# A graph, mixer and wavelet layer on one core: edge pairs spread over 24 mlp turns, finishing steps begun with the last of them, and a 512-wide product in three one-pass parts

## The chip, the cores and the metric

One core of a Trainium2 chip runs the whole layer. The metric is the device time of one execution in microseconds. Engines are named PE (matmul), DVE (vector), ACT (scalar), POOL (GpSimd) and SP (the queue that issues plain DMAs). Each engine works through its own list in order, and engines wait for each other by semaphores.

## The reference, cut to what matters

The layer has 6250 rows of 512 numbers and 100,000 edges from `dst` to `src`.

```python
xn = layernorm(x)
hidden = relu(xn @ W1 + b1)                     # graph part, 256 wide
h = hidden @ W2 + b2
x = x + h + segment_sum(h[dst], src) + mixer(xn)   # mixer: random-feature attention, then
                                                   # an mlp: gelu(norm(y) @ w1 + b1) @ w2 + b2
ll = haar_low_band(layernorm(x))
delta = fc2(gelu(fc1(interp(ll)))) - ll
x = x + layernorm(x) + haar_inverse_of(delta)
```

As `h` is linear behind the relu, the kernel sums `hidden` over the edges first and multiplies the sums by `W2` once for each row.

## The kernel before

The 6250 rows stand in 125 partitions, 50 tiles; a step is two tiles, so each pass over the rows has 25 steps (`STEPS`). Pass 1 computes keys, the `hidden` rows (stored to DRAM as the table `hidden_rows`) and sorts the edges. The sorted edges are then worked off in 440 pairs (`PAIRS`), each a pair of 128 edges that belong to one tile of 125 rows. For a pair POOL issues two indirect DMAs (`gathers`, L609), which fetch 2 x 128 rows of the table into one of 12 places of a ring (`RING`); ACT makes 0/1 matrices from the edges' row numbers (`one_hots`, L1272 and L1276, four pairs at a time); PE multiplies (`groups`, L876 to L879); DVE adds the result to the tile's sums in `acc` (`add_groups`, L1732). These four do their work between the steps of passes 2 and 3, so many pairs at each place of a step.

Pass 2 (attention, step 2 in what follows) has 25 steps with 8 pairs each. After it comes a loop over turns v. In turn v the mlp of step a = v is computed as long as there is one (`transposes` L970, `features` L983, `mlp2` L992 on PE; `norm_rows` L1292, `gelus` and `copy_hT` L1182 on ACT; `skip_rows` L1856, L1858 and `z_rows` L1866 on DVE), and step b = v - `LAG` is finished, when there is one. In the finishing of a step its sums are transposed (`acc_transposes`, L1016), copied by ACT (`copy_accT`, L1327), multiplied by `W2` (`w2_products` L1024 into banks that are free while mlp turns run, later `x1_products` L1057, which adds onto what `x1_opened`, L1049 and L1051, has put into the bank); DVE takes the row statistics (`x1_rows`, L1890 to L1897), POOL the inverse roots (`roots`, L618), DVE the low band (`ll_rows`, L1903 to L1917); then follow `ll_transposes` (L1067), `fc1` (L1075), `fc2` (L1085), ACT's `scaled_rows` (L1350) and DVE's `out_rows` (L1925, L1931). A turn works on three steps at once: it transposes and multiplies the sums of step b + 2 (b + 1 in mlp turns), takes the statistics of step b + 1 and finishes step b.

`pair_counts` deals the pairs to the turns. Step t may be finished once 390 + 2t + 2 pairs are in. Before, 22 turns of 8 bring 176 pairs, so that `LAG` is 23: turns 0 to 21 are mlp alone, turns 22, 23 and 24 are mixed (mlp and finishing), turns 25 to 47 are the tail, finishing alone (b = 2 to 24). Turns 22 to 24 have 8 pairs too, the first six of the tail 4 each. In POOL's list a turn's `gathers` stand before its `roots`:

```python
gathers(TURN + sum(SECOND) + BETWEEN + sum(THIRD[:v]) + soon + RING)
if 0 <= b + 1 < STEPS:
    roots(steps[b + 1])
```

## Time and profile before

| | |
|---|---|
| three runs | 1779.51, 1782.45, 1791.55 us; median 1782.45 us |
| the profiled execution | 1781.86 us, span 1780.0 us |
| granted TensorE clock, mean | 0.969 of full speed |
| pass 2, steady steps | about 600 to 980 us |
| mlp turns 0 to 21 | about 1016 to 1470 us |
| mixed turns 22 to 24 | about 1470 to 1568 us |
| tail turns, b = 2 to 24 | about 1569 to 1780 us |

A timeline row gives start and length in us from the start of the span, the engine, the source line, the operation and its output and inputs; in brackets stands how long the engine had been idle and who released it. "PE" rows of fp32 matmuls count two for each matmul written in the code. A turn is told by its first row of one kind: the copy `L1182` marks mlp turns (late in the turn), the transposes `L1067` the start of a tail turn.

### The profile page before, as it was taken

The page shows a single profiled execution, that of the slowest core. Times are in us where ns is not written, and L with a number is a line of the kernel's source. Part 1 is how long each engine was busy: PE and PEld are TensorE (multiplying, and loading weights), DVE is VectorE, ACT ScalarE, POOL GpSimd, SP SyncE. Part 2 cuts the span into 40 slices and gives each one's busy share as a digit, 9 for nine tenths or more (in the row PEclk, how much of TensorE's full clock was granted, in tenths as well). Part 3 has the DMA queues.
Part 4 walks back from the last instruction along what each step waited for, and adds up shares of the span by engine and source line. Part 5 has one row for each costly group of instructions (what it writes and reads, how often), then busy time and mean ns, then how long its engine had stood idle before and what let it go on. Part 6 is the DMA issues. An engine that isn't in the chain of part 4 may idle for free.

```text
span 1780.0 us, 24848 instructions
## 1 busy us (share of the span) xinstructions
PE 1625.4 (91%) x8131; PEld 1224.3 (69%) x8131; DVE 1035.9 (58%) x2321; ACT 818.5 (46%) x1890; POOL 1036.6 (58%) x1129
## 2 busy tenths in 40 slices
PE   4999999998899999999999699999999988789996
PEld 3778877787677788888877476666666665556554
DVE  5899999996255555565565233333333334357776
ACT  2135444444244344554454465555554554435442
POOL 3023444343777777777777777777777777553010
PEclk9999999999899999999999699999999999889998
DMA  6023222222356556656655755555565655444332
GB/s 191 12 75 123 87 87 87 87 88 89 114 156 202 175 173 189 184 177 187 185 177 150 233 170 169 187 172 179 176 183 178 181 180 172 130 136 141 127 131 81
DMA packets 87425, 263.61 MB, mean 148 GB/s; under 512 B 18765, under 2 KB 20813, under 8 KB 87298
## 3 DMA queue, kind: packets, MB, share of 16 engines
q0 software_dynamic: 43456, 119.44, 24.1%
q1 hardware_dynamic: 43842, 142.59, 23.6%
q8 instruction: 67, 1.10, 0.2%
q14 instruction: 60, 0.49, 0.1%
HBM read 217.15 MB, written 44.80 MB: 147 GB/s over the span
## 4 chain that ended last, share of the span: by engine, by line
PE 49%; POOL 15%; DVE 14%; issue 9%; DMA 8%; ACT 3%; DVEq 0%; POOLq 0%; ACTq 0%
POOL sb_weights L609 12%; PE bank L983 6%; DVE sb_weights L1452 6%; DMA sb_weights<-hidden_rows,sb_weights 5%; PE bank L992 5%; PE bank L931 4%; PE bank L901 2%; PE bank L903 2%; PE bank L902 2%; PE bank L1057 2%; PE turn_bank L877 2%; PE bank L877 2%; DMA sb_step<-x_t 2%; DVE sb_step L1633 2%; PE bank L726 1%
## 5 line engine op out<-in xcount | busy, mean ns | idle before, releaser
L609 POOL DMA_INDIRECT sb_weights<-hidden_rows,sb_weights x880 | 862.0, 980 | 298.8 <-issue 244.4
L1732 DVE TENSOR_TENSOR sb_acc<-sb_acc,bank 125x257 f32 x220 | 92.6, 421 | 345.6 <-PE bank L879 301.5
L1272 ACT ACTIVATE sb_weights<-sb_const,sb_weights 128x125 f16<-128x125 f16 x880 | 266.5, 388 | 50.9 <-PE turn_bank L879 49.7
L992 PE MATMUL bank<-sb_weights,sb_step 128*125 128x512 f32 x400 | 188.4, 616 | 10.0 <-issue 8.5
L983 PE MATMUL bank<-sb_weights,sb_step 128*128 128x250 f32 x800 | 184.8, 384 | 10.3 <-issue 8.0
L983 PEld LDWEIGHTS bank<-sb_weights,sb_step 128*128 128x128 f32 x800 | 151.1, 194 | 33.3 <-issue 15.6
L1452 DVE TENSOR_TENSOR sb_weights<-sb_weights 128x512 f32<-128x512 f32 (+3 forms) x256 | 164.3, 683 | 3.6
L1732 DVE TENSOR_TENSOR sb_acc<-sb_acc,turn_bank 125x257 f32 x220 | 92.5, 420 | 107.1 <-PE turn_bank L879 85.9
L576 POOL TENSOR_SCALAR sb_const<-sb_const 125x2 f32<-125x2 f32 x25 | 9.5, 381 | 240.0 <-ACT sb_step L1174 240.0
L1190 ACT ACTIVATE sb_step<-sb_step 125x256 f32<-125x256 f32 x100 | 48.2, 502 | 215.3 <-DVE sb_step L1625 214.7
L725 PE MATMUL bank<-sb_w_parts,sb_x_high 128*125 128x512 f32 (+1 forms) x400 | 139.0, 348 | 0.0
L992 PEld LDWEIGHTS bank<-sb_weights,sb_step 128*125 128x125 f32 x400 | 74.3, 195 | 89.0 <-issue 86.9
L726 PE MATMUL bank<-sb_w_parts,sb_x_high 128*125 128x512 f32 (+1 forms) x400 | 135.1, 338 | 0.0
L727 PE MATMUL bank<-sb_w_parts,sb_x_low 128*125 128x512 f32 (+1 forms) x400 | 134.9, 337 | 0.0
L1276 ACT ACTIVATE sb_weights<-sb_weights,sb_const 128x1000 f16<-128x1000 f16 x110 | 124.1, 1128 | 3.6
L738 PE MATMUL bank<-sb_w_parts,sb_x_high 128*125 128x256 f32 (+1 forms) x300 | 102.7, 342 | 16.7 <-DVE sb_step L1633 14.1
L1306 ACT COPY sb_step<-bank 128x500 f32<-128x500 f32 x25 | 14.4, 576 | 190.5 <-PE bank L919 190.5
L618 POOL TENSOR_TENSOR sb_step<-sb_step,sb_const 125x2 f32<-125x2 f32 x25 | 17.5, 698 | 142.7 <-DVE sb_step L1897 142.6
L931 PE MATMUL bank<-sb_const,sb_step 128*125 128x512 f32 x200 | 95.6, 601 | 0.0
L876 PE MATMUL turn_bank<-sb_weights 128*125 128x257 f16 x220 | 63.0, 287 | 35.4 <-DMA sb_weights<-hidden_rows,sb_weights 29.0
L739 PE MATMUL bank<-sb_w_parts,sb_x_high 128*125 128x256 f32 (+1 forms) x300 | 94.6, 315 | 0.0
L740 PE MATMUL bank<-sb_w_parts,sb_x_low 128*125 128x256 f32 (+1 forms) x300 | 94.6, 315 | 0.0
(310 smaller groups left out, 3632.2 us busy)
## 6 DMA issues: line engine op xcount, KB each, us to landing
sb_step<-x SPq DMA_DIRECT2D x63, 500.0 KB
sb_step<-x_t SPq DMA_DIRECT2D x50, 500.0 KB, 6.7
sb_weights<-hidden_rows,sb_weights POOLq DMA_INDIRECT x880, 4.5
y_rows<-sb_step SPq DMA_DIRECT2D x25, 500.0 KB
sb_step<-y_rows SPq DMA_DIRECT2D x25, 500.0 KB
z_rows<-sb_step SPq DMA_DIRECT2D x25, 500.0 KB
sb_weights<-z_rows SPq DMA_DIRECT2D x13, 500.0 KB
out<-sb_weights SPq DMA_DIRECT2D x13, 500.0 KB
```

The lines of the kernel that those rows point to most:

```text
L609: pool.indirect_dma_start(out=ring[:, n % RING * 2 + h, 0:HID], out_offset=None, in_=table, in_offset=bass.IndirectOffsetOnAxis(ap=row_of[ ...
L725: pe.matmul(bk, high, rhs(0, c), start=c == 0, stop=False)
L726: pe.matmul(bk, high, rhs(1, c), start=False, stop=False)
L727: mm = pe.matmul(bk, low, rhs(0, c), start=False, stop=c == KC - 1)
L738: pe.matmul(outs[c], high, first, start=c == 0, stop=False)
L931: mm = pe.matmul(banks[m][0:P, :], qpT[:, c, m * P:(m + 1) * P], pmat[:, c, :], start=False, stop=c == KH - 1)
L983: last = pe.matmul(bk[:, (c % 2) * 250:(c % 2) * 250 + 2 * P], mlp1_w[:, k, c * 128:(c + 1) * 128], hT3[:, t.s, k, :], start=k == 0, stop= ...
L992: mm = pe.matmul((BC, BD)[m][0:P, :], gT3[:, k, m * P:(m + 1) * P], mlp2_w[:, k, :], start=k == 0, stop=k == KC - 1)
L1272: mm = act.activation(hit[q % 2][:, i, :], iota_h[:, :], ACT.Abs, bias=less_lane[:, q * BP + i // 2, i % 2:i % 2 + 1])
L1276: act.activation(hit[q % 2], hit[q % 2], ACT.Relu, scale=-1.0, bias=one_c[:, 0:1]).then_inc(hits, 1)
L1452: sort_op(dve.tensor_tensor(half(target, c, lo), a, b, op))
L1732: dve.tensor_tensor(dst, dst, (BE, BH)[n % 2][0:P, 0:RW], ALU.add).then_inc(g_add, 1)
```

## The change

Three things are changed.

1. The 176 pairs that must be in before a step can be finished are spread over 24 turns of seven or eight pairs (7, 7, 8, 7, 7, 8, ...), so `LAG` is 25. Turns 0 to 23 are mlp alone, turn 24 is the one mixed turn and only begins finishing (b = -1: sums of steps 0 and 1, statistics and low band of step 0), and turns 25 to 49 are the tail, b = 0 to 24. Turn 24 has 8 pairs, the first ten turns of the tail 4 each. ACT makes the 0/1 matrices by a rule (`hits_until`) instead of two batches a turn.
2. The product of the sums with `W2` is made of one-pass products (fp32 data read as F32R): the weights are split once into a high and a low part (`late_weights`), the sums in each step: ACT's copy becomes the high part, and a new DVE instruction `sums_low` subtracts it from the bank for the low part. PE then does high x high, high x low and low x high, 12 instructions of 512 columns in place of 4 full fp32 matmuls.
3. PE waits for the low part (`a_low`) where it waited for the copy (`a_t`): before the product, and before `fc2`, whose bank is the one that the sums were read from. Tiles move to other places (`fc1e`, `fc2_w`, `t4`, `accT`), and `fc2_w` is loaded one wait later.

```diff
 def pair_counts():
     turn, second, between = 8, [8] * STEPS, 8
-    start, third, lag = turn + sum(second) + between, [], 1
-    while start + sum(third) < PAIRS - NT + 2:
-        third.append(min(8, PAIRS - NT + 2 - start - sum(third)))
-    lag = len(third) + 1
+    start, lag = turn + sum(second) + between, STEPS
+    third = spread(PAIRS - NT + 2 - start, lag - 1)
     while start + sum(third) < PAIRS:
         third.append(min(8 if len(third) < STEPS else 4, PAIRS - start - sum(third)))
...
-SLOT = [0, 1, 2, 0, 6] + [(5, 4, 3, 1, 2, 0, 6)[u % 7] for u in range(STEPS - 5)]
+SLOT = [(0, 1, 2, 6, 5, 4, 3)[u % 7] for u in range(STEPS)]
...
+            def sums_product(bk, m, opened):
+                for c in range(KH):
+                    high, low = (v[:, c, m * P:(m + 1) * P].bitcast(F32R) for v in (accT, acc_low))
+                    w_high, w_low = (v[:, c, :].bitcast(F32R) for v in (gnn2_high, gnn2_low))
+                    pe.matmul(bk, high, w_high, start=c == 0 and not opened, stop=False)
+                    pe.matmul(bk, high, w_low, start=False, stop=False)
+                    mm = pe.matmul(bk, low, w_high, start=False, stop=c == KH - 1)
+                return mm
...
             def x1_products(t):
-                pe.wait_ge(a_t, t.u + 2)
+                pe.wait_ge(a_low, t.u + 2)
                 for m in (0, 1):
-                    for c in range(KH):
-                        mm = pe.matmul(x1_of(t, m), accT[:, c, m * P:(m + 1) * P], gnn2_w[:, c, :],
-                                       start=False, stop=c == KH - 1)
+                    mm = sums_product(x1_of(t, m), m, True)
                 mm.then_inc(a_mm, 1)
...
             def fc2(t):
...
                 if t.u + LAG >= STEPS:
-                    pe.wait_ge(a_t, min(STEPS, t.u + 3) + 1)
+                    pe.wait_ge(a_low, min(STEPS, t.u + 3) + 1)
...
+            def hits_until(n):
+                while next_hits[0] < BATCHES and BP * (next_hits[0] - 1) <= n:
+                    one_hots(next_hits[0])
...
                     gelus(steps[a], 0)
-                    one_hots(2 * STEPS + 5 + 2 * a)
+                    hits_until(ahead)
...
                     gelus(steps[a], 1)
-                    one_hots(2 * STEPS + 6 + 2 * a)
+                    hits_until(ahead + sum(counts[0:2 if a == 2 else 3]))
...
+            def sums_low(t):
+                dve.wait_ge(a_t, t.u + 2)
+                dve.tensor_tensor(acc_low.rearrange("p a b -> p (a b)").bitcast(F32R), sums_bank(t)[:, 0:500],
+                                  accT.rearrange("p a b -> p (a b)"), ALU.subtract).then_inc(a_low, 1)
...
                     if b + 1 < STEPS:
                         x1_rows(steps[b + 1])
+                    if b + 2 < STEPS:
+                        sums_low(steps[b + 2])
                     add_groups(counts[0] + counts[1])
```

POOL, from the first gather to the fourth of its `roots` (the line of `roots` is L618 before and L621 after; 812 gathers are 406 pairs). Before:

```order
L609 DMA sb_weights<-hidden_rows,sb_weights 128x256 x812
L618 TENSOR_TENSOR sb_step<-sb_step,sb_const 125x2
L609 DMA sb_weights<-hidden_rows,sb_weights 128x256 x16
L618 TENSOR_TENSOR sb_step<-sb_step,sb_const 125x2
L609 DMA sb_weights<-hidden_rows,sb_weights 128x256 x16
L618 TENSOR_TENSOR sb_step<-sb_step,sb_const 125x2
L609 DMA sb_weights<-hidden_rows,sb_weights 128x256 x12
L618 TENSOR_TENSOR sb_step<-sb_step,sb_const 125x2
```

and after:

```order
L612 DMA sb_weights<-hidden_rows,sb_weights 128x256 x812
L621 TENSOR_TENSOR sb_step<-sb_step,sb_const 125x2
L612 DMA sb_weights<-hidden_rows,sb_weights 128x256 x12
L621 TENSOR_TENSOR sb_step<-sb_step,sb_const 125x2
L629 COPY sb_step<-sb_const 128x125 x2
L632 COPY sb_step<-sb_acc 125x2
L612 DMA sb_weights<-hidden_rows,sb_weights 128x256 x8
L621 TENSOR_TENSOR sb_step<-sb_step,sb_const 125x2
```

The same 812 gathers stand ahead of the first roots; behind them 16, 16, 12 and three times 8 have become 12 and seven times 8.

PE, a tail turn without gathers, from its first transposes into the product (before):

```order
L1067 MATMUL bank2<-sb_const,sb_step 128x125 x2
L1016 MATMUL bank1<-sb_const,sb_acc 128x125 x4
L1049 MATMUL bank0<-sb_weights,sb_step 125x512
L1075 MATMUL bank2<-sb_step,sb_weights 128x125 x4
L1049 MATMUL bank3<-sb_weights,sb_step 125x512
L1085 MATMUL bank1<-sb_weights,sb_step 125x256 x2
L1031 MATMUL bank2<-sb_const,sb_step 126x125 x2
L1057 MATMUL bank0<-sb_weights 125x512 x2
L1057 MATMUL bank3<-sb_weights 125x512 x2
```

and after:

```order
L1019 MATMUL bank1<-sb_const,sb_acc 128x125 x4
L1059 MATMUL bank0<-sb_weights,sb_step 125x512
L1083 MATMUL bank2<-sb_step 128x125 x4
L1059 MATMUL bank3<-sb_weights,sb_step 125x512
L1093 MATMUL bank1<-sb_step 125x256 x2
L1041 MATMUL bank2<-sb_const,sb_step 126x125 x2
L1027 MATMUL bank0<-sb_w2_parts 125x512
L1028 MATMUL bank0<-sb_w2_parts 125x512
L1029 MATMUL bank0<-sb_w2_parts 125x512
```

The order is the same; the four full products at the end are now the three rows L1027 to L1029, four times over (twice for bank0, twice for bank3).

DVE, a tail turn without gathers, from the statistics to the low band (before):

```order
L1890 BN_STATS sb_const<-bank5 125x6
L1890 BN_STATS sb_const<-turn_bank 125x6
L1892 TENSOR_SCALAR sb_const<-sb_const 1x1
L1894 BN_AGGR sb_step<-sb_const 125x2 x2
L1897 TENSOR_SCALAR sb_step<-sb_step 125x2
L1903 SCALAR_TENSOR_TENSOR sb_step<-sb_step 125x2
L1905 TENSOR_SCALAR sb_step<-sb_step 125x2
```

and after:

```order
L1911 BN_STATS sb_const<-bank5 125x6
L1911 BN_STATS sb_const<-turn_bank 125x6
L1913 TENSOR_SCALAR sb_const<-sb_const 1x1
L1915 BN_AGGR sb_step<-sb_const 125x2 x2
L1918 TENSOR_SCALAR sb_step<-sb_step 125x2
L1897 TENSOR_TENSOR sb_w2_parts<-bank1,sb_w2_parts 128x500
L1924 SCALAR_TENSOR_TENSOR sb_step<-sb_step 125x2
```

The subtraction of `sums_low` (after: L1897) stands where DVE hands the variances to POOL and next waits for POOL's roots.

## Rows read from the trace of the kernel before

**Rows 1.** The page: busy time of each engine, share of the span

```profile
PE 1625.4 (91%) x8131; PEld 1224.3 (69%) x8131; DVE 1035.9 (58%) x2321; ACT 818.5 (46%) x1890; POOL 1036.6 (58%) x1129
```

**Rows 2.** The gathers (L609) in two stretches: window, length, busy us, count, PEclk, DMA, GB/s

```profile
1034.00:1259.67 225.67, 172.06 (x177) 0.98 0.58 177
1259.67:1466.88 207.21, 157.85 (x163) 0.98 0.60 179
```

**Rows 3.** What PE waited for, 1180 to 1460 us: total, times, longest

```profile
PE turn_bank L876 <- DMA sb_weights<-hidden_rows,sb_weights: 18.9, 13, 2.2
```

**Rows 4.** Timeline, hT copies of mlp turns 0, 1, 2 and 21: start, length, engine

```profile
1034.01 0.57 ACT L1182 COPY sb_weights<-bank 128x500 f32<-128x500 f32 x1 [4.59 <-PE bank L970]
...
1052.51 0.57 ACT L1182 COPY sb_weights<-bank 128x500 f32<-128x500 f32 x1 [4.59 <-PE bank L970]
...
1079.16 0.57 ACT L1182 COPY sb_weights<-bank 128x500 f32<-128x500 f32 x1 [8.53 <-PE bank L970]
...
1466.88 0.57 ACT L1182 COPY sb_weights<-bank 128x500 f32<-128x500 f32 x1 [6.29 <-PE bank L970]
```

**Rows 5.** Timeline, turns 22 to 24, the mixed ones

```profile
1493.76 0.74 POOL L618 TENSOR_TENSOR sb_step<-sb_step,sb_const 125x2 f32<-125x2 f32 x1
...
1494.53 0.16 DVE L1903 SCALAR_TENSOR_TENSOR sb_step<-sb_step 125x2 f32<-125x2 f32 x1 [11.21 <-POOL sb_step L618]
...
1498.20 0.44 PE L876 MATMUL bank<-sb_weights 128*125 128x257 f16 x1 [6.84 <-DVE sb_acc L1732]
...
1518.63 2.04 PE L992 MATMUL bank<-sb_weights,sb_step 128*125 128x512 f32 x2 [4.23 <-issue]
...
1568.17 1.04 PE L1016 MATMUL bank<-sb_const,sb_acc 125*128 125x125 f32 x4
```

**Rows 6.** Timeline, the start of tail turns 2, 6, 8 and 23

```profile
1578.77 0.38 PE L1067 MATMUL bank<-sb_const,sb_step 125*128 125x125 f32 x2
...
1621.49 0.38 PE L1067 MATMUL bank<-sb_const,sb_step 125*128 125x125 f32 x2
...
1642.06 0.38 PE L1067 MATMUL bank<-sb_const,sb_step 125*128 125x125 f32 x2
...
1760.09 0.38 PE L1067 MATMUL bank<-sb_const,sb_step 125*128 125x125 f32 x2
```

**Rows 7.** Timeline, POOL's roots in tail turns 2, 3 and 4

```profile
1580.89 0.71 POOL L618 TENSOR_TENSOR sb_step<-sb_step,sb_const 125x2 f32<-125x2 f32 x1 [8.29 <-DVE sb_step L1897]
...
1593.62 0.72 POOL L618 TENSOR_TENSOR sb_step<-sb_step,sb_const 125x2 f32<-125x2 f32 x1 [0.71 <-DVE sb_step L1897]
...
1604.81 0.72 POOL L618 TENSOR_TENSOR sb_step<-sb_step,sb_const 125x2 f32<-125x2 f32 x1
```

**Rows 8.** Timeline, tail turn 9, without gathers (1649.94 to 1657.82 us)

```profile
1650.78 0.57 ACT L1327 COPY sb_weights<-bank 128x500 f32<-128x500 f32 x1
...
1651.80 0.17 DVE L1897 TENSOR_SCALAR sb_step<-sb_step 125x2 f32<-125x2 f32 x1
...
1652.77 0.16 DVE L1903 SCALAR_TENSOR_TENSOR sb_step<-sb_step 125x2 f32<-125x2 f32 x1 [0.80 <-POOL sb_step L618]
...
1653.20 1.13 PE L1085 MATMUL bank<-sb_weights,sb_step 128*125 128x256 f32 x4
...
1654.39 3.60 PE L1057 MATMUL bank<-sb_weights 128*125 128x512 f32 x8
...
1658.02 1.30 DVE L1890 BATCH_NORM_STATS2 sb_const<-bank 125x6 f32<-125x512 f32 x2 [0.67 <-PE bank L1057]
```

**Rows 9.** Timeline, one-pass matmuls in step 2, and a sum from PSUM

```profile
722.56 0.40 PE L902 MATMUL bank<-sb_w_parts,sb_x_high 128*125 128x512 f32 x1
...
724.87 0.40 PE L903 MATMUL bank<-sb_w_parts,sb_x_low 128*125 128x512 f32 x1
...
1477.39 0.69 DVE L1886 TENSOR_TENSOR sb_weights<-sb_weights,bank 125x512 f32<-125x512 f32 x1 [4.59 <-PE turn_bank L1024]
```

**Rows 10.** Timeline, rows of an mlp turn that wait for a load

```profile
1281.60 1.52 ACT L1292 ACTIVATE sb_step<-sb_step,sb_const 125x512 f32<-125x512 f32 x2 [0.51 <-DMA sb_step<-y_rows]
```

40 lines of the change are left out of this document (25 added, 15 removed).

## The prediction

> **What bounds the kernel now.** I read the page first: PE is busy 91% of the span and every other engine under 60% [rows 1]. So PE sets most of the time, and the question is where it doesn't. The waits by stage and the timeline turn by turn give three regimes.
>
> In the mlp turns PE waits for gathered rows: 18.9 us in 13 waits between 1180 and 1460 us [rows 3]. POOL issues them without a pause, 163 in 207.21 us, that is 1.271 us each or 2.54 us a pair [rows 2]; the stretch before has 1.275. Eight pairs are 20.3 us. Turns 0 to 21 take (1466.88 - 1034.01) / 21 = 20.6 us each [rows 4]. Where enough rows lie ready a turn with eight pairs takes 18.50 us (turn 0 to turn 1), and turn 2, with its extra products for the fc weights, 26.65 us [rows 4]. POOL's issue rate is the bound here, and PE has 2 us to spare a turn.
>
> In the mixed turns the engines wait for each other. POOL computes the first roots only behind its 812th gather, at 1493.8 us; DVE has by then waited 11.21 us for them, and PE, which waits for DVE's adds, 6.84 us [rows 5]. In the next turn PE stands 4.23 us behind ACT (the gelu of `fc1` is queued behind a batch of 0/1 matrices) [rows 5]; turn 24 shows the same. The end of turn 22 lies at about 1499.9 us (PE resumes at 1498.2 and has two pairs' products, eight of 0.44 us overlapping by half). From there to 1568.17 us, where the last mlp turn ends [rows 5], two turns take 68.3 us.
>
> In the tail, turns without pairs last (1760.09 - 1642.06) / 15 = 7.87 us [rows 6], and PE is full: its eight product rows alone start at 1654.39 and DVE gets them at 1658.02 [rows 8]. DVE needs 7.21 of these 7.87 us (it idles 0.67 at the end of its turn), 0.80 of it waiting for roots [rows 8]. Turns with pairs are longer: where POOL still gathers, its roots are 1604.81 - 1593.62 = 11.19 us apart (8 x 1.27 us of gathers and 1.0 us for roots and the degree copy) [rows 7]; behind the last gather the two turns from 1621.49 to 1642.06 us take 10.28 us each [rows 6].
>
> **The change, part by part.**
>
> *Two more pure mlp turns in the same time.* The gathers that stand ahead of POOL's first roots are the same 812, so that point stays at 1493.8 us unless PE becomes later than POOL. From the mark of turn 0 to the mark of the last pure turn there were 168 pairs; there are 169 now, since the marks stand behind the third of a turn's four places. At 2.54 us that is 429 us, and the measured 432.9 holds some start-up. PE on its own needs at most 23 x 18.50 + 8.15 (turn 2) = 433.7 us for them, less for the 16 turns with seven pairs. Both ways the mark of turn 23 falls at 1467 us, where turn 21 has it now. The extra mlp work goes into the 2 us a turn that PE waits today. Turn 24 then is what turn 22 was, and even 5 us of lateness would vanish in the 6.84 us stall. The 0/1 matrices: I went through the batches turn by turn; each is asked for at least one place ahead of its use, so I count nothing. The weights' split adds a copy and a subtraction of 1024 columns on DVE in turn 3, at most four times the 0.69 us of a subtraction of 512 [rows 9]; even if PE waited for all of it, POOL would run ahead meanwhile and the time come back later: nothing.
>
> *Two mixed turns gone.* -68.3 us.
>
> *The passage into the tail.* Before it takes 1578.77 - 1568.17 = 10.6 us from the transposes of the sums to the first tail mark [rows 5, 6]. Now DVE must do `sums_low` ahead of the `add_b2` that PE waits for: transposes 1.04, copy 0.57, subtraction 0.69 [rows 5, 8, 9], with the hand-overs 2.4 us where DVE could start after 0.8: +1.6. The cheaper product gives back about 0.8. So 11.4 us (bounds 9 and 14), and the first mark (b = 0) is at 1499.9 + 11.4 = 1511.3 us.
>
> *Tail turns with pairs: ten instead of six, and POOL behind.* Roots of turn b = 0 come 2.1 us behind the mark (1580.89 - 1578.77 [rows 6, 7]): 1513.4 us. The next need 12.0 us (12.73 less 0.71 of idle [rows 7]): 1525.4. Six more gaps of 11.19 bring the roots of b = 7 to 1592.5 us. The mark of the next turn follows 5.5 us later (1604.81 + 11.19 to 1621.49): b = 8 at 1598.0. Two turns of 10.28 with pairs but no gathers: b = 10 at 1618.6 us. The shorter product gives nothing in these ten turns, since POOL or the circle through ACT's matrices sets them; `sums_low` costs nothing either: fc2, its first reader, comes behind two of the turn's pairs. If the roots and gathers overlapped better the floor is 10.28 a turn, -6 us in all; if `sums_low` were on the path, +0.7 a turn.
>
> *Tail turns without pairs.* One-pass matmuls follow each other 2.31 / 10 = 0.231 us apart [rows 9]; twelve take 2.8 us in place of 3.44 (eight rows, 3.60 with the last one's end [rows 8]). PE's turn goes from 7.87 to 7.22. `sums_low` has the size of the 0.69 us subtraction in [rows 9]. The copy that it waits for starts at 1650.78 and is long done when DVE has its variances out, 1651.97; it then fits into the 0.80 us that DVE waits for POOL, and ends at 1652.7, 0.5 us before fc2 (1653.20) and 1.7 before the product (1654.39) [rows 8]. DVE's chain of 7.21 us is then as long as PE's: I take 7.26 us (bounds 7.21 and 7.90). Thirteen turns from b = 10 to b = 23: 94.4 us, mark b = 23 at 1713.0 us.
>
> The Trainium skill, page "FP8 and Floating Point Precision", section "TensorE Precision Notes", says that true fp32 takes four passes through the array. The 0.86 us of such a matmul against 0.231 for one pass agrees roughly. By the page three of four passes would be 2.58 us, PE's turn 7.01, and DVE's 7.21 would set it, 0.6 us less over thirteen turns.
>
> *Sum.* Mark b = 23 moves from 1760.09 to 1713.0: -68.3 for the mixed turns, +0.8 for the passage, and 201.7 us for 23 tail turns in place of 181.3 for 21, +20.4; together -47.1 us. What follows that mark (19.9 us of span) has no product and stays. The profiled execution took 1781.86 us, 0.6 under the median of 1782.45: 1781.9 - 47.1 = **1735 us**, 2.6% less.
>
> **Rivals.**
>
> *The low half is not hidden (1749 us).* POOL's answer could come 0.7 us later because the variances are handed over no earlier, or the waits around the new instruction add up: DVE's chain is then 7.90 us and sets 13 turns, +8.3 us, and the eight POOL-bound turns get 0.7 each, +5.6. For it: DVE has no slack left in my sum. Against: the gap of 0.80 us is there in each of the turns.
>
> *The parts don't pay (1743 us).* Here the change doesn't do what it says: high and low weights alternate, and twelve instructions take the 3.44 us of before. +0.61 x 13 = 8 us. Against it: [rows 9] are the same pattern with the same widths.
>
> *The mlp turns keep their 20.6 us (1760 us).* The y rows of the next step arrive only as ACT asks for them (0.51 us of idle at 1281.6 [rows 10]); the load waits for a store of the turn before, and with 18.6 us a turn it would come up to 2 us later against PE. If that held every turn at 20.6, turn 23's mark would move by 41 us; turn 24 would then need PE's own 21 us and not 33, -12, and POOL, with rows in hand, would give the tail some 4 us: 1735 + 25. For it: the load is late today. Against: ACT's rows are used first 2 us later, and the turn of 18.50 us shows that the loads can follow.
>
> *Slower (1805 us).* fc2 now waits for `a_low`, which stands on DVE behind the statistics of the step before, which wait for the product of the turn before. That closes a circle product, statistics, low half, fc2, product. By the rows it has 0.5 us to spare in each turn. If the low half came 3.3 us later than I read (behind the adds of the pairs, or a copy of ACT queued behind its matrices), each of 25 turns would grow by 2.8 us: +70. The circle decides from 0.5 us of lateness on, and the kernel as a whole becomes slower at 1.9 us a turn. Against: in turns with pairs the copy precedes the matrices in ACT's list, and `sums_low` precedes the adds.
>
> **How the numbers follow.** Forecast 0.68, low half not hidden 0.15, parts don't pay 0.05, mlp turns unchanged 0.08, slower 0.04. The range takes from the forecast down to 1722 (10.28 us in seven turns -7, passage -2, and some 4 for the mark of turn 23 being earlier) and up to 1758 (7.90 us turns +8, pairs' turns +6, a late turn 24 +7). A measurement of this kernel can tell about 1% from no change, 1764.6 us: the first three cases and a part of the fourth are faster, 0.90; the rest of the fourth is the same, 0.06; slower 0.04.
>
> **What the profile after would show.** Right: PE's waits for gathered rows in the mlp turns nearly gone, marks 18.6 us apart, turn 23's at 1467; one long wait of DVE for roots near 1494; roots 11.2 us apart until about 1592; tail turns without pairs near 7.26 us with DVE and PE both full; twelve one-pass rows 0.23 us apart. Wrong: marks still 20 us apart with ACT waiting for y rows, PE idle before fc2, or POOL idle between 1034 and 1494, which would mean that PE holds the ring and not POOL.

## The result and the profile after

The changed kernel takes 1735.8 us, the median of four runs (1731.9 to 1744.8), beside 1783.9 us for the kernel before on the same chip: a ratio of 0.9734, 95% interval 0.9689 to 0.9778. The forecast was 1735 us. The profiled execution took 1733.5 us, 1731.5 of them the span. In the profile after, line numbers are higher by 3 to 21: the gathers stand in L612, POOL's roots in L621, the copies of hT in L1190, the tail's marks in L1075, the product's three parts in L1027 to L1029, `sums_low` in L1897.

The page, its row of the engines and two of its groups, which answer to [rows 1] and [rows 2]:

```profile
span 1731.5 us, 25102 instructions
PE 1600.6 (92%) x8243; PEld 1240.8 (72%) x8243; DVE 1045.1 (60%) x2340; ACT 817.4 (47%) x1892; POOL 1036.6 (60%) x1131
...
L612 POOL DMA_INDIRECT sb_weights<-hidden_rows,sb_weights x880 | 862.4, 980 | 281.8 <-issue 248.7
...
L995 PE MATMUL bank<-sb_weights,sb_step 128*125 128x512 f32 x400 | 179.8, 592 | 1.4 <-ACT sb_step L1401 1.4
```

PE is busy 92% of a span that is 48.5 us shorter. `mlp2` (L995) idles 1.4 us in all; before (L992) it was 10.0 us, two waits of 4.23 us in the mixed turns among them.

PE's waits between 1180 and 1460 us, which answer to [rows 3], in the view of the waits (engine, line, what it waited for, us in total, times, longest):

```profile
PE bank L986 <- issue: 12.2, 14, 2.3
```

The 18.9 us of waits for gathered rows are gone. In their place stands a wait ahead of `features`, 12.2 us in 14 times (2.5 us in two before), with a releaser that this view doesn't name. The code and ACT's timeline point to it, and feature_wait_2 below tests it:

```profile
1116.04 0.57 ACT L1190 COPY sb_weights<-bank 128x500 f32<-128x500 f32 x1 [4.59 <-PE bank L973]
...
1119.89 1.52 ACT L1304 ACTIVATE sb_step<-sb_step,sb_const 125x512 f32<-125x512 f32 x2 [2.80 <-DMA sb_step<-y_rows]
1121.31 0.81 ACT L1332 ACTIVATE sb_step<-bank,sb_const 128x250 f32<-128x250 f32 x2
```

The second half of a step's features waits until both gelus of the first half are out (`feat_c`). They stand on ACT behind the normalized rows of the next step, and those stood 2.80 us behind the load of the y rows, so the gelus start 5.3 us after the first copy of hT.

The copies of hT at the end of turns 0, 1, 2 and 23, which answer to [rows 4]:

```profile
1033.51 0.57 ACT L1190 COPY sb_weights<-bank 128x500 f32<-128x500 f32 x1 [0.71 <-PE bank L973]
...
1052.00 0.57 ACT L1190 COPY sb_weights<-bank 128x500 f32<-128x500 f32 x1 [0.28 <-PE bank L973]
...
1078.62 0.57 ACT L1190 COPY sb_weights<-bank 128x500 f32<-128x500 f32 x1 [8.53 <-PE bank L973]
...
1474.40 0.57 ACT L1190 COPY sb_weights<-bank 128x500 f32<-128x500 f32 x1 [4.59 <-PE bank L973]
```

From turn 0 to turn 23 the mean is (1474.40 - 1033.51) / 23 = 19.2 us: quicker than the 20.6 us of before with its eight pairs. Both means hold the long turn 2. Without its 26.62 us the others take 18.8 us each, where 18.6 was forecast, and none of them takes less than 18.49 us, with seven pairs or with eight.

POOL's timeline at its first roots and in the tail, which answers to [rows 5, 7], and the rows of DVE and PE that wait behind the first ones:

```profile
1494.27 0.74 POOL L621 TENSOR_TENSOR sb_step<-sb_step,sb_const 125x2 f32<-125x2 f32 x1
...
1512.31 0.72 POOL L621 TENSOR_TENSOR sb_step<-sb_step,sb_const 125x2 f32<-125x2 f32 x1 [1.92 <-DVE sb_step L1918]
...
1525.05 0.73 POOL L621 TENSOR_TENSOR sb_step<-sb_step,sb_const 125x2 f32<-125x2 f32 x1 [0.70 <-DVE sb_step L1918]
...
1580.89 0.73 POOL L621 TENSOR_TENSOR sb_step<-sb_step,sb_const 125x2 f32<-125x2 f32 x1
...
1592.07 0.73 POOL L621 TENSOR_TENSOR sb_step<-sb_step,sb_const 125x2 f32<-125x2 f32 x1
```

```profile
1495.04 0.16 DVE L1924 SCALAR_TENSOR_TENSOR sb_step<-sb_step 125x2 f32<-125x2 f32 x1 [4.84 <-POOL sb_step L621]
...
1498.72 0.30 PE L879 MATMUL bank<-sb_weights 128*125 128x257 f16 x1 [1.33 <-DVE sb_acc L1745]
```

The first roots come at 1494.27 us, DVE has waited 4.84 us for them, and PE 1.33 us for DVE's next add. Behind them the roots of the tail's turns with pairs are 11.18 us apart, and between 1525 and 1592 us POOL waits for another engine 0.7 us in all: it is full.

The tail's marks on PE, which answer to [rows 6]: b = 0, 8, 10, 11 and 23.

```profile
1510.20 0.38 PE L1075 MATMUL bank<-sb_const,sb_step 125*128 125x125 f32 x2
...
1596.95 0.38 PE L1075 MATMUL bank<-sb_const,sb_step 125*128 125x125 f32 x2
...
1617.62 0.38 PE L1075 MATMUL bank<-sb_const,sb_step 125*128 125x125 f32 x2
...
1625.37 0.38 PE L1075 MATMUL bank<-sb_const,sb_step 125*128 125x125 f32 x2
...
1711.91 0.38 PE L1075 MATMUL bank<-sb_const,sb_step 125*128 125x125 f32 x2
```

And a turn without pairs, which answers to [rows 8]: DVE's timeline, two of the product's twelve rows on PE, and the windows view of twelve such turns (us; busy time and instructions of PE, PEld, DVE, ACT and POOL; PE's granted clock; DMA share; GB/s).

```profile
1656.27 0.67 DVE L1897 TENSOR_TENSOR sb_w_parts<-bank,sb_w_parts 128x500 fp32r<-128x500 f32 x1
1657.17 0.16 DVE L1924 SCALAR_TENSOR_TENSOR sb_step<-sb_step 125x2 f32<-125x2 f32 x1 [0.22 <-POOL sb_step L621]
```

```profile
1652.94 0.39 PE L1027 MATMUL turn_bank<-sb_w_parts 128*125 128x512 f32 x1
1653.17 0.40 PE L1028 MATMUL turn_bank<-sb_w_parts 128*125 128x512 f32 x1
```

```profile
1625.40:1711.90 86.50, 86.50 (x431) 63.46 (x430) 80.72 (x206) 40.18 (x83) 9.75 (x23) 1.00 0.32 129
```

PE is busy for all of the 86.5 us. The product's rows follow each other 0.23 us apart, as in [rows 9]. `sums_low` lies where DVE waited for the roots; 0.22 us of that wait is left.

### The profile page after: what moved, and what is told of

Its sections match the earlier page's. It is cut to its first block, busy times and chain, and to the rows that moved or that the text cites. A ratio compares the mean times of both kernels' runs of the same rounds, so it can differ in the third digit from the quotient of the medians.

```text
span 1731.5 us, 25102 instructions
## 1 busy us (share of the span) xinstructions
PE 1600.6 (92%) x8243; PEld 1240.8 (72%) x8243; DVE 1045.1 (60%) x2340; ACT 817.4 (47%) x1892; POOL 1036.6 (60%) x1131
## 4 chain that ended last, share of the span: by engine, by line
PE 55%; DVE 14%; issue 13%; POOL 13%; ACT 3%; DMA 3%; DVEq 0%; POOLq 0%; ACTq 0%
PE bank L986 10%; PE bank L995 9%; POOL sb_weights L612 8%; DVE sb_weights L1465 6%; PE bank L934 4%; PE bank L904 2%; PE bank L905 2%; PE bank L906 2%; PE turn_bank L880 2%; PE bank L880 2%; PE bank L728 2%; PE bank L729 2%; PE bank L730 2%; DVE sb_step L1646 1%; PE turn_bank L879 1%
## 5 line engine op out<-in xcount | busy, mean ns | idle before, releaser
L612 POOL DMA_INDIRECT sb_weights<-hidden_rows,sb_weights x880 | 862.4, 980 | 281.8 <-issue 248.7
L1280 ACT ACTIVATE sb_weights<-sb_const,sb_weights 128x125 f16<-128x125 f16 x880 | 266.6, 389 | 70.5 <-PE turn_bank L882 70.1
L995 PE MATMUL bank<-sb_weights,sb_step 128*125 128x512 f32 x400 | 179.8, 592 | 1.4 <-ACT sb_step L1401 1.4
L1284 ACT ACTIVATE sb_weights<-sb_weights,sb_const 128x1000 f16<-128x1000 f16 x110 | 124.1, 1128 | 3.6
L995 PEld LDWEIGHTS bank<-sb_weights,sb_step 128*125 128x125 f32 x400 | 71.2, 187 | 74.3 <-issue 72.5
L835 PE MATMUL bank<-sb_step 125*128 125x256 f32 x400 | 90.8, 380 | 1.1 <-ACT sb_step L1258 1.1
L880 PE MATMUL turn_bank<-sb_weights 128*125 128x256 f16 x440 | 85.6, 277 | 0.0
```

What stands on the lines that cost most here:

```text
L612: pool.indirect_dma_start(out=ring[:, n % RING * 2 + h, 0:HID], out_offset=None, in_=table, in_offset=bass.IndirectOffsetOnAxis(ap=row_of[ ...
L880: mm = pe.matmul(bk[0:P, 0:HID], one_hot, row[:, HIGH], start=False, stop=False)
L995: mm = pe.matmul((BC, BD)[m][0:P, :], gT3[:, k, m * P:(m + 1) * P], mlp2_w[:, k, :], start=k == 0, stop=k == KC - 1)
L1280: mm = act.activation(hit[q % 2][:, i, :], iota_h[:, :], ACT.Abs, bias=less_lane[:, q * BP + i // 2, i % 2:i % 2 + 1])
L1284: act.activation(hit[q % 2], hit[q % 2], ACT.Relu, scale=-1.0, bias=one_c[:, 0:1]).then_inc(hits, 1)
```

## The experiments

Twelve kernels ran, four at a time beside the kernel before. The groups fell on three chips. The first two groups ran on chips on which the kernel before takes 1979 and 1977 us; the third on one like that of the prediction, 1784 us. Ratios are to the kernel before on the same chip; two kernels of different groups are compared across chips.

| kernel | before, us | this, us | ratio, 95% interval |
|---|---|---|---|
| e1_deal_only | 1979.0 | 1958.2 | 0.9884 (0.9855 to 0.9913) |
| e2_parts_only | 1979.0 | 1970.1 | 0.9963 (0.9939 to 0.9988) |
| e3_feature_wait | 1979.0 | 1939.0 | 0.9807 (0.9776 to 0.9838) |
| e5_low_twice | 1979.0 | 1957.8 | 0.9890 (0.9860 to 0.9920) |
| after_again | 1977.3 | 1948.6 | 0.9854 (0.9807 to 0.9901) |
| e4_half_gathers | 1977.3 | 1933.7 | 0.9776 (0.9734 to 0.9819) |
| e6_tail_threes | 1977.3 | 1946.6 | 0.9829 (0.9782 to 0.9876) |
| e7_tail_twos | 1977.3 | 1943.3 | 0.9820 (0.9772 to 0.9868) |
| after_third | 1784.1 | 1739.1 | 0.9755 (0.9733 to 0.9776) |
| feature_wait_2 | 1784.1 | 1736.5 | 0.9741 (0.9719 to 0.9763) |
| e8_twos_split | 1784.1 | 1730.2 | 0.9685 (0.9661 to 0.9709) |
| e9_all | 1784.1 | 1722.4 | 0.9652 (0.9632 to 0.9671) |

To compare tails I use the time from the second roots of POOL (step 1) to the last (step 24), which is 23 tail turns: 1714.09 - 1512.31 = 201.8 us in the changed kernel.

### e1_deal_only

```diff
-                pe.wait_ge(a_low, t.u + 2)
+                pe.wait_ge(a_t, t.u + 2)
                 for m in (0, 1):
-                    mm = sums_product(x1_of(t, m), m, True)
+                    for c in range(KH):
+                        mm = pe.matmul(x1_of(t, m), accT[:, c, m * P:(m + 1) * P], gnn2_w[:, c, :],
+                                       start=False, stop=c == KH - 1)
```

The same in `w2_products`; `fc2` waits for `a_t`; `sums_low` and the weights' parts are left out.

> The changed kernel with the product of the sums as before: two matrix products of full fp32 rows, no low half, no parts of the weights. Only the deal of the pairs and the later start of the finishing steps are left. Theory (the terms of the prediction): two mixed turns less, -68.3 us; passage as before, 0; tail turns 0 to 10 as in the changed kernel, since POOL's gathers and roots pace them; thirteen turns without pairs at 7.87 us instead of 7.23, so the mark of turn 23 is 13 x 0.64 = 8.3 us later than in the changed kernel: about 1743 us, ratio to before 0.977 to 0.978. Rival (the three parts also shorten the turns with pairs, because PE or the circle through the product sets them and not POOL): ten more turns lose up to 0.6 us each, 1749 us or more, and POOL's roots would stand 11.8 us apart in place of 11.18.

POOL's timeline, roots of two neighbouring turns without pairs:

```profile
1880.46 0.69 POOL L621 TENSOR_TENSOR sb_step<-sb_step,sb_const 125x2 f32<-125x2 f32 x1 [7.06 <-DVE sb_step L1919]
1888.34 0.69 POOL L621 TENSOR_TENSOR sb_step<-sb_step,sb_const 125x2 f32<-125x2 f32 x1 [7.06 <-DVE sb_step L1919]
```

Turns without pairs take 7.88 us, as before the change. Turns with pairs are 11.0 to 12.7 us apart (mean of the seven from 1746.02 to 1829.34: 11.9), in the changed kernel on such a chip 11.0 to 13.2 (1742.78 to 1828.08: 12.2). The turn behind 1746.02 takes 11.16 us with the full product, as the changed kernel's on the first chip. So the three parts shorten only the turns without pairs, 13 x 0.68 = 9 us, as the theory had it, and the rival falls, as far as a chip shows it on which these turns vary by 2 us. The ratio that the theory named, 0.977, is not that of this chip; against after_again it is 0.003 higher, where 0.005 was to be seen, and the intervals overlap.

### e2_parts_only

```diff
-    start, lag = turn + sum(second) + between, STEPS
-    third = spread(PAIRS - NT + 2 - start, lag - 1)
+    start, third, lag = turn + sum(second) + between, [], 1
+    while start + sum(third) < PAIRS - NT + 2:
+        third.append(min(8, PAIRS - NT + 2 - start - sum(third)))
+    lag = len(third) + 1
```

`SLOT` is that of the kernel before again.

> The changed kernel with the old deal: eight pairs in each mlp turn, finishing steps from the 23rd turn on, and the product in three one-pass parts with the low half on DVE. Theory: fifteen turns without pairs at 7.23 us in place of 7.87, -9.6 us; the passage +0.8; POOL paces the rest: 1783.9 - 9 = 1775 us, ratio 0.995. Rival (the low half lengthens the circle product, statistics, low half, fc2 in the mixed turns): the three mixed turns grow by 0.7 us each or more, 1777 to 1780 us, ratio 0.996 to 0.998, and the mixed turns, 68.3 us for two before, are longer than 69.5.

The fifteen turns without pairs take 7.10 to 7.27 us (roots of POOL) in place of 7.87, and the median is 8.9 us lower: the theory's -9. The theory's ratio of 0.995 and the rival's 0.996 to 0.998 both lie in the interval. The first roots of POOL stand 24.1, 32.9 and 34.9 us apart; I have no mixed turns of the kernel before from such a chip to set beside them, so whether `sums_low` lengthens these stays open. The two halves of the change add up: 20.8 us in e1_deal_only and 8.9 here are 29.7 us, and the whole change gives 28.8 on the second chip of this speed (after_again). How the 48 us on the first chip divide was not run.

### e3_feature_wait and feature_wait_2

```diff
-                pe.wait_ge(feat_c, t.g * 2 + i + 1)
+                pe.wait_ge(feat_c, t.g * 2 + 1)
```

> The changed kernel, but the second half of a step's features no longer waits for the first half's gelus of the same step; it waits, as its bank needs, for the gelus of the step before. Theory (the gelus stand on ACT behind the rows of the next step, which wait for the y rows; that cost 0.6 us a turn and up to 2.3, and nothing else made the mlp turns 19.17 us instead of 18.6): marks of the hT copies 18.1 to 18.7 us apart, turn 23's mark at 1462 to 1469 us instead of 1474.4, and the whole time unchanged within 2 us, because POOL's first roots at 1494 us hold the mixed turn: ratio 0.972 to 0.974. Rival (the late y rows hold the turn itself): the wait only moves to the transposes of the next step, marks stay 19.1 us apart. Second rival (PE holds POOL's ring back): POOL's first roots come earlier than 1494 by up to 4 us and the whole time falls by as much.

> The kernel with the earlier features again, now beside the changed kernel. On a chip like the first: theory (POOL's first roots at 1494 us, behind 812 gathers, hold the mixed turn, so PE's earlier arrival only makes its wait longer) hT marks at 18.1 to 18.7 us apart, turn 23's mark at 1462 to 1469 us, the whole within 2 us of the changed kernel; rival (PE held the ring, and so POOL) 4 us or more less. On a chip like the second the ring is held by PE: POOL's waits for the ring fall from the 60 us of the changed kernel, and the whole by 8 to 15 us.

On the third chip, beside the changed kernel, PE's waits from 1033 to 1456 us and the hT copies of turns 0 and 23 of feature_wait_2:

```profile
PE turn_bank L879 <- DMA sb_weights<-hidden_rows,sb_weights: 12.4, 14, 1.6
```

```profile
1032.85 0.58 ACT L1190 COPY sb_weights<-bank 128x500 f32<-128x500 f32 x1 [0.72 <-PE bank L973]
...
1464.11 0.58 ACT L1190 COPY sb_weights<-bank 128x500 f32<-128x500 f32 x1 [4.27 <-PE bank L973]
```

The wait ahead of `features` is gone altogether, and where rows lie ready turns with seven pairs take 17.7 us. A turn of the changed kernel with seven pairs takes 18.5 us or more, so that wait cost 0.8 us even where it was short, and the rival that the late y rows hold the turn falls. But PE now waits for gathered rows again, 12.4 us in 14 times, and the mean is (1464.11 - 1032.85) / 23 = 18.75 us. PE is 10 us earlier at turn 23 than in the first profile of the changed kernel, POOL's first roots stand at 1495.31 us as there (1494.27), and PE now waits 12.66 us behind them. The whole takes 1736.5 beside 1739.1 us, 2.7 us less where the theory had at most 2, within the intervals of each other: the theory's reading. On the chip of the first group e3 has the lowest ratio, and between 1115 and 1675 us POOL's waits for the ring (PE's pairs, L882) are 36 us where after_again, on another chip, has 59 us. The intervals of 0.9807 and 0.9854 overlap, so a gain there is likely, not shown; the ratio of 0.972 to 0.974 that the theory named is not that of this chip.

### e5_low_twice

```diff
             def sums_low(t):
                 dve.wait_ge(a_t, t.u + 2)
+                if t.u > 2:
+                    seq(dve.tensor_tensor(acc_low.rearrange("p a b -> p (a b)").bitcast(F32R), sums_bank(t)[:, 0:500],
+                                          accT.rearrange("p a b -> p (a b)"), ALU.subtract))
                 dve.tensor_tensor(acc_low.rearrange("p a b -> p (a b)").bitcast(F32R), sums_bank(t)[:, 0:500],
```

> The changed kernel with the subtraction of the low half done twice, one behind the other, from step 3 on (the result is the same). Theory (the low half lies in the wait for POOL's roots, of which 0.2 us a turn are left): in turns without pairs DVE's chain of 7.2 us grows by 0.5 us or more, thirteen turns of 7.7 to 8.0 us instead of 7.23, +6 to +10 us; turns with pairs stay at 11.18 us, since POOL sets them: 1742 to 1746 us, ratio 0.976 to 0.979. Rival (the circle product, statistics, low half, fc2 has no slack either in turns with pairs): these grow by 0.7 us too, together +13 to +16 us, 1749 to 1752 us. Rival on the other side (DVE has slack that I don't see): no change, 1736 us.

DVE's timeline in a turn without pairs:

```profile
1890.15 0.17 DVE L1921 TENSOR_SCALAR sb_step<-sb_step 125x2 f32<-125x2 f32 x1
1890.23 0.67 DVE L1898 TENSOR_TENSOR sb_w_parts<-bank,sb_w_parts 128x500 fp32r<-128x500 f32 x1
1890.93 0.68 DVE L1900 TENSOR_TENSOR sb_w_parts<-bank,sb_w_parts 128x500 fp32r<-128x500 f32 x1
1891.53 0.15 DVE L1927 SCALAR_TENSOR_TENSOR sb_step<-sb_step 125x2 f32<-125x2 f32 x1
```

The second subtraction comes 0.70 us behind the first, the 0.22 us of wait for POOL is gone, and the roots of POOL are 7.50 us apart in all thirteen turns. That is +0.24 to +0.4 us on the 7.11 to 7.26 us of the changed kernel, 4 us over the thirteen turns and not 6 to 10: DVE had 0.3 to 0.46 us to spare a turn and not 0.2, since PE and not DVE set these turns. Turns with pairs are as they were (11.2 to 13.0 us). The cover of the low half is thus nearly used up: a longer one would cost at once.

### after_again

> The changed kernel as it stands, beside the other kernels of this group, because the chip of the first four kernels ran the kernel before in 1979 us instead of 1784: its POOL stopped for 2.5 us about every sixth gather in the mlp turns, each time with a releaser outside the engines. Theory (POOL's pace with the gathers sets the mlp turns, and the change gains only what it takes out behind them): on such a chip the ratio is 0.985 to 0.990, about 1953 us, and the turns with pairs in the tail alternate between 11.2 and 12 to 13 us. On a chip like the first, 0.9734 again, within 0.968 to 0.978.

The ratio is the one that the theory named: 0.9854. But POOL is not what is stopped on this chip. Three of the waits from 1121 to 1690 us of after_again, and a stretch of its timeline:

```profile
DVE sb_acc L1745 <- remote: 130.9, 39, 7.6
...
POOL sb_weights L612 <- remote: 61.0, 34, 2.8
...
POOL sb_weights L612 <- PE bank L882: 43.5, 21, 5.7
```

```profile
1184.16 0.57 ACT L1190 COPY sb_weights<-bank 128x500 f32<-128x500 f32 x1 [3.29 <-remote]
...
1184.38 0.42 DVE L1745 TENSOR_TENSOR sb_acc<-sb_acc,bank 125x257 f32 x1 [1.70 <-remote]
1184.52 0.94 POOL L612 DMA_INDIRECT sb_weights<-hidden_rows,sb_weights  x1 [2.02 <-remote]
```

No profile from the chips of 1784 us has a "remote" row, a releaser that the profile places on none of the engines. By the code all three instructions wait for PE: the copy of hT for its transposes, the add and the gather for its pairs. In 32 of POOL's 34 stops DVE's add has the same mark and starts 0.14 us ahead of the gather. In the stretch shown PE's transposes for the copy stand at 1180.53 us and the copy starts 3.6 us behind them, where in the changed kernel's first profile it is 0.6 us (1134.31 and 1134.94). So on this chip PE's results come late, up to some 3 us, and POOL, DVE and ACT wait for them together. Between such stops POOL's gathers start 1.25 us apart as on the first chip. PE's granted clock is 0.94 of full speed over the mlp turns and 0.93 between 600 and 980 us, where the changed kernel's first profile has 1.00 in both; so for a part of the time it stands at 1.2 GHz, the lower of its two levels, and that is part of the loss. Turn 0's mark stands at 1162.39 us, 129 us later, and the 23 turns from there to turn 23's take 526.7 us in place of 440.9. Roots of the tail's turns with pairs are 11.0 to 13.2 us apart. What makes PE's results late the profile doesn't say.

### e4_half_gathers

```diff
-                    for h in (0, 1):
+                    for h in (0, 1)[0:1 if n >= 400 + RING else 2]:
                         pool.indirect_dma_start(
...
-                    pe.wait_ge(gathered[n % RING], 32 * (n // RING + 1))
+                    pe.wait_ge(gathered[n % RING], 32 * (n // RING + 1) - 16 * max(0, (n - 400) // RING))
```

> The changed kernel without the second gather of the pairs 412 to 439, 28 gathers fewer; the second rows of these pairs are what lay there before, so their sums are other ones. All work of PE, DVE and ACT is unchanged. Theory (POOL's eight gathers and its roots set the tail's turns with pairs, 11.18 us each): from the third of them on they fall to what PE, DVE and ACT need among themselves, 10.28 us as in the two turns behind the last gather: six to seven turns x 0.9 us, -5 to -6.5 us on a chip like the first, up to -12 us where gathers stall. Rival (PE, which is busy 9.3 us of these 11.2, and the waits for ACT's scaled rows set them): under 2 us less. Turns without pairs stay at 7.23 us by both.

POOL's timeline, two roots in the turns with pairs:

```profile
1757.74 0.72 POOL L621 TENSOR_TENSOR sb_step<-sb_step,sb_const 125x2 f32<-125x2 f32 x1 [1.96 <-DVE sb_step L1918]
...
1767.98 0.72 POOL L621 TENSOR_TENSOR sb_step<-sb_step,sb_const 125x2 f32<-125x2 f32 x1 [1.84 <-DVE sb_step L1918]
```

They are 10.24 us apart in place of the neighbour's 11.0 to 13.2 (mean of eight 12.3), and the idle time before them is a wait for DVE. Turns without pairs didn't move (7.11 to 7.26). So with half of these gathers left out the turns with pairs fall to the next limit, 10.3 us. The 23 turns take 199.4 us in place of 212.0, the whole 15 us less, with intervals that still overlap by 0.001. The ends predicted were -5 and -12. Two things went at once, though: the tail of this profile has no "remote" row either, where after_again has eleven behind 1730 us. What POOL alone costs is better read beside the 201.8 us of the first chip, which has none: 2.4 us, since the turns of 11.18 us there end in one of 8.12 us that catches up. That POOL holds the turns with pairs is thus shown, by its full timeline there and by this run; that it costs more than some 2 us in the tail is not. In the remaining waits PE stands 1.2 to 1.3 us for ACT's scaled rows in five of eight turns.

### e6_tail_threes and e7_tail_twos

```diff
-        third.append(min(8 if len(third) < STEPS else 4, PAIRS - start - sum(third)))
+        third.append(min(8 if len(third) < STEPS else 2, PAIRS - start - sum(third)))
...
-                if a >= STEPS and next_hits[0] < BATCHES:
+                while a >= STEPS and next_hits[0] < BATCHES and BP * next_hits[0] < ahead + sum(THIRD[v:v + 2]):
                     one_hots(next_hits[0])
```

(`3` in place of `2` in e6_tail_threes.)

> The changed kernel, but the last 40 pairs are dealt out three a turn over fourteen tail turns instead of four a turn over ten, and ACT computes a batch of 0/1 matrices only in the turn before its first use. Theory (POOL sets the turns with four pairs, PE those without): a turn with three pairs needs 6 x 1.26 + 1.0 = 8.6 us of POOL and 9.25 - 0.45 = 8.8 us of PE, with the waits for ACT 9.5 at most; 13.3 turns of 8.8 to 9.5 and 9.7 of 7.23 are 187 to 197 us instead of 201.7: -5 to -14 us, ratio to the changed kernel 0.992 to 0.997. Rival (the circle between PE, ACT and DVE sets any turn that has pairs, at 10.3 us): 13.3 x 10.3 + 70 = 207, +5 us.

> As the kernel with three pairs a turn, but with two: twenty tail turns with two pairs each. Theory: PE needs 7.23 + 2 x 0.45 = 8.1 us a turn, POOL 6.0; 20 x 8.1 to 8.8 and 3 x 7.23 are 184 to 198 us instead of 201.7: -4 to -18 us. Rival (any turn with pairs takes 10.3 us): 20 x 10.3 + 22 = 228, +26 us. If two and three pairs a turn come out alike and faster than four, PE's total work sets the tail once POOL doesn't.

With three pairs the turns take 9.4 to 10.5 us (one 8.8), and all 23 take 202.2 us, in place of the neighbour's 212.0. The turn was forecast at 8.8 to 9.5 and is longer, but not the rival's 10.3 throughout. With two pairs the turns alternate. PE's timeline of e7_tail_twos has the reason, and ACT's what stands in front:

```profile
1803.76 1.02 PE L1059 MATMUL bank<-sb_step 126*125 126x512 f32 x2
...
1813.59 1.09 PE L1059 MATMUL bank<-sb_step 126*125 126x512 f32 x2 [1.59 <-ACT sb_step L1362]
```

```profile
1801.78 1.45 ACT L1362 ACTIVATE sb_weights<-bank,sb_step 125x512 f32<-125x512 f32 x2 [1.34 <-DVE sb_step L1935]
...
1808.40 2.43 ACT L1280 ACTIVATE sb_weights<-sb_const,sb_weights 128x125 f16<-128x125 f16 x8
...
1811.90 0.76 ACT L1362 ACTIVATE sb_step<-bank,sb_step 125x512 f32<-125x512 f32 x1
```

In the turn without a batch of 0/1 matrices ACT's scaled rows start at 1801.78 and PE opens the next product at 1803.76 with no wait: 8.0 us. In the next the batch (L1280 and L1284, 3.5 us) stands in front, the scaled rows come at 1811.90, and PE waits 1.59 us: 9.9 us. The 23 turns take 199.5 us. So behind POOL the next limit is the order of ACT's queue, not PE's work. By the whole times, 0.9829 and 0.9820 beside 0.9854, the intervals overlap. Here too most of the gain on the neighbour lies in PE's late results, with no "remote" row in the tail of e7 and two in that of e6: on the first chip the tail with four pairs takes 201.8 us, against which three pairs give nothing and two 2.3 us.

### after_third and e8_twos_split

```diff
             def one_hots(q, between=lambda: None):
...
                 mm.then_inc(hits, 1)
+                between()
                 act.wait_ge(hits, q * 2 + 2)
...
+                if a >= STEPS:
+                    degrees = (lambda: copy_degrees(steps[b + 3])) if b + 3 < STEPS else (lambda: None)
+                    if next_hits[0] < BATCHES and BP * next_hits[0] < ahead + sum(THIRD[v:v + 2]):
+                        one_hots(next_hits[0], degrees)
+                    else:
+                        degrees()
```

e8_twos_split has the deal of two pairs a turn of e7_tail_twos besides.

> The changed kernel a third time, as the measure for the three kernels beside it. On a chip like the first (kernel before at 1784 us, gathers 1.28 us apart without stops) 1735 us, ratio 0.969 to 0.978; on one like the second (1977 us, stops of 2 us and more between gathers) 0.981 to 0.990.

> Two pairs a turn in twenty tail turns, as before, and ACT's batch of 0/1 matrices cut in two there: its eight first instructions (2.4 us) ahead of the copy of the degrees, the last (1.1 us) behind it, so that it ends before the scaled rows can start. Theory (of the two kinds of turns, 8.0 us without a batch and 9.9 with one, the second is long because the scaled rows stand behind the batch and PE's next opening product behind them): all twenty turns 8.0 to 8.4 us; from the roots of the second step to those of the last 183 to 191 us in place of 199.5, and 201.8 with four pairs a turn on the first chip. On a chip like the first 1719 to 1726 us, ratio to the changed kernel about 0.992. Rival (with the batch earlier, the degrees' copy comes late and the gelus' reader waits): turns with a batch stay over 9.3 us, gain under 3 us against two pairs without the cut.

after_third stayed in its range, 0.9755. Its profiled execution was the longest of its five, 1747.7 us, and has its first roots late, in POOL's timeline, with PE's wait behind them:

```profile
1506.56 0.72 POOL L621 TENSOR_TENSOR sb_step<-sb_step,sb_const 125x2 f32<-125x2 f32 x1
```

```profile
1510.99 0.45 PE L879 MATMUL bank<-sb_weights 128*125 128x257 f16 x1 [10.25 <-DVE sb_acc L1745]
```

The mlp turns are no slower there (turn 23's copy at 1477.75 us), but POOL had issued 448 gathers between 400 and 1034 us in place of 453 and 313 in place of 317 up to 1440 us. Nine gathers are 11.5 us, and the roots are 12.3 us late. The first five are lost before 620 us, where POOL waits 16.3 us for PE's pairs in place of 10.8; the others in the mlp turns, where a gather takes 993 ns in place of 977. From the first roots to the end of the span it is 237.2, 239.3 and 238.6 us in the three profiles of this tail (after, after_third, feature_wait_2): the moment at which POOL's 812 gathers are out carries the difference between executions to the end.

e8_twos_split: with the batch cut in two, turns with and without one take 8.04 us from step 2 to step 11. The roots of POOL, twice in such turns, and then where it ends:

```profile
1591.99 0.72 POOL L621 TENSOR_TENSOR sb_step<-sb_step,sb_const 125x2 f32<-125x2 f32 x1
...
1600.08 0.72 POOL L621 TENSOR_TENSOR sb_step<-sb_step,sb_const 125x2 f32<-125x2 f32 x1
...
1609.96 0.72 POOL L621 TENSOR_TENSOR sb_step<-sb_step,sb_const 125x2 f32<-125x2 f32 x1
```

```profile
1609.05 1.12 PE L1059 MATMUL bank<-sb_step 126*125 126x512 f32 x2 [1.31 <-DMA sb_step<-z_rows]
```

From 1600 us on six turns take 8.9 to 9.9 us, since PE's opening product waits 0.6 to 1.7 us for the load of the z rows: as I read it, the turns have become shorter than a store and a load on one slot of z; I didn't try it with more slots. The 23 turns take 192.3 us, just past the 183 to 191 of the theory, and the whole 1730.2 us, past its 1719 to 1726. The ratio to the changed kernel is 0.9685 / 0.9755 = 0.993; the two intervals don't meet. The rival (turns with a batch over 9.3 us) falls for the first ten turns.

### e9_all

```diff
-                gathers(TURN + sum(SECOND) + BETWEEN + sum(THIRD[:v]) + soon + RING)
+                gathers(TURN + sum(SECOND) + BETWEEN + sum(THIRD[:v]) + soon + RING - (3 if v == STEPS - 1 else 0))
```

with the edits of e8_twos_split and feature_wait_2.

> The kernel with two pairs a turn and the cut batch, and both ends of the way into it: the features' earlier wait, and POOL's first roots behind 806 gathers instead of 812. Theory: each frees what the other holds. On a chip like the first PE reaches the mixed turn some 6 us earlier and finds the roots 7.7 us earlier, at about 1487 us; the whole falls by 4 to 7 us against the kernel with two pairs and the cut, to 1713 to 1720 us. Rival (the roots wait for the variances on DVE, which are out at 1487 us only): POOL idles ahead of its first roots, and the gain is under 3 us.

POOL's first roots, and DVE's row behind them:

```profile
1490.61 0.74 POOL L621 TENSOR_TENSOR sb_step<-sb_step,sb_const 125x2 f32<-125x2 f32 x1
```

```profile
1491.38 0.16 DVE L1927 SCALAR_TENSOR_TENSOR sb_step<-sb_step 125x2 f32<-125x2 f32 x1 [8.58 <-POOL sb_step L621]
```

1722.4 us: 0.9652 to the kernel before, 16.7 us less than the changed kernel beside it (1739.1) and 7.8 less than e8_twos_split, against 4 to 7 expected; the interval of e8_twos_split overlaps by 0.001. The 1713 to 1720 us and the roots at 1487 us that the theory named were not reached. DVE still waits 8.58 us for the roots, so POOL doesn't idle ahead of them, and the rival falls: the roots could move up further. Of the two edits neither is shown alone here; the features' wait alone gave 2.7 us, within the noise.

## Why the prediction was right, and where it wasn't

The sum came out step by step, and not only in total.

- *POOL as the anchor.* "That point stays at 1493.8 us": 1494.27. after_third and the roots-to-end times of three profiles show that this moment sets the end, and so does feature_wait_2, where PE comes 10 us earlier and gains next to nothing.
- *Two more mlp turns in the same time.* This is the step that failed in size: 18.6 us a turn and turn 23's mark at 1467 us; measured 18.8 us (turn 2 left out) and 1474.40. The sum took 18.50 us as PE's own time for eight pairs, "less for the 16 turns with seven pairs"; measured, no turn with seven is shorter than 18.49. The reason is the wait of `features` for gelus that are queued on ACT behind the rows that wait for the y load, 19.1 us in 21 waits from 1033 to 1456 us in the profile after. feature_wait_2 takes it away, and its turns with seven pairs take 17.7 us. The y rows were in the rivals, but as a load that holds every turn at 20.6 us. I argued that ACT's rows "are used first 2 us later" and missed that the gelus of the current step stand behind them. It cost nothing, since lateness vanishes in the stall at POOL's roots, as the text said. But that stall, which it took at 6.84 us with room for five, was 1.33 us on PE: 7.4 us of lateness all but used it up, and that the total still came out is in part luck.
- *Two mixed turns gone, and the passage.* First mark 1511.3 forecast, 1510.20 measured.
- *Tail turns with pairs.* Roots of b = 0, 1, 7 at 1513.4, 1525.4, 1592.5 forecast; 1512.31, 1525.05, 1592.07 measured; 11.18 us apart. POOL's timeline, with 0.7 us of waits in six turns, and e4_half_gathers show that it is POOL that holds them, and e1_deal_only that the shorter product gives nothing there, as the forecast said.
- *Tail turns without pairs.* 7.26 us forecast; the first took 7.75 us (`fc2` waited 0.44 us for `sums_low` there, the one such wait), the mean of the others is (1711.91 - 1625.37) / 12 = 7.21. e1_deal_only takes 7.88. That DVE's chain "is then as long as PE's" was too strict: e5_low_twice shows some 0.4 us of slack on DVE, which leaves a chain of 7.50 - 0.70 = 6.8 us. By the Trainium skill's page "FP8 and Floating Point Precision", section "TensorE Precision Notes", true fp32 takes four passes; the turn with three passes in place of four is shorter by 0.66 us of the 3.44 us (19%), where that rule gives a quarter, 0.86. The trace agrees roughly; DVE's chain of 6.8 us would have left room for all of it.
- *The sum.* Last mark at 1713.0 forecast, 1711.91 measured; behind it 19.6 us in place of 19.9.
- *The rivals.* Low half not hidden: no (0.22 us of wait left, e5). Parts that don't pay: no, twelve rows 0.23 us apart. mlp turns kept at 20.6: no, though the late y rows were at work, with 7.4 us at turn 23's mark where the rival had 41. The circle that makes it slower: PE, on which `fc2` would wait for `a_low`, is busy in all of the 86.5 us.
- *The range.* Its upper end doesn't follow from its terms: 1735 + 8 + 6 + 7 is 1756 and not 1758. Nothing else hangs on it.

What the forecast could not know is the chip: where PE's results come late (after_again), the same change gives 1.5% and not 2.7%. There 1735 us would have been far off, though the direction holds.

## What to carry to other kernels

Find the engine whose work must all be issued before a given point (here 812 gathers before the first roots) and keep it as a clock: work moved ahead of that point is free only up to the stall that it leaves, and the time behind it can be summed on its own. Where a wait goes, look at the order of the queue on each engine that feeds the next one. Here twice a short piece of work that the next matmul needed (gelus, scaled rows) stood behind a longer one that could wait, and 16.7 us more came from spreading, cutting and moving, with no work taken away.

## What the runs showed of the hardware that I had not expected

- Chips differ by a large amount. On two of the chips the kernel before took 1977 to 1979 us in place of 1784. In after_again POOL, DVE and ACT stand together behind results of PE that come up to some 3 us late, 34 times in 569 us by POOL's rows, and PE's granted clock is 0.94 there. A tail turn without pairs still takes 7.1 to 7.27 us on all of the chips, and neither e4_half_gathers nor e7_tail_twos, with fewer gathers a turn, has such a stop in its tail. Whether the gathers bring them about was not tested.
- The number of gathers issued in a stretch also differs a little between executions at the same speed (453 and 448 in the same 634 us, through waits for PE's pairs), and with four more lost in the mlp turns that carries to the first roots as 12 us.
- A subtraction of 500 columns into the parts takes 0.67 us, and the one behind it starts 0.70 us later though it waits for a semaphore: the hand-over costs 0.03 us beyond the instruction itself.
